# A two-layer attention kernel on one Trainium2 core: the last step's exponentials added by a transfer, a new order in layer 0, another layout of layer 1's q and k

## What is computed

```python
xn = layernorm(x)                                    # layer 0
scores = einsum('bhsd,bhtd->bhst', q, k) * scale     # q, k, v projections of xn
attn = softmax(scores, axis=-1)                      # no bias in layer 0
out = einsum('bhst,bhtd->bhsd', attn, v)             # then the projection WO[0]
x = x + out_projected * silu(ffn(xn))
xn = layernorm(x)                                    # layer 1
q, k = rope(q, c, s), rope(k, c, s)                  # halves of the head's 64 rotated
scores = einsum('bhqd,bhkd->bhqk', q, k) * SCALE
kb = -p * log1p(a * dist)
attn = softmax(scores + kb[None], axis=-1)
out = einsum('bhqk,bhkd->bhqd', attn, v)
x = x + (out @ out_w.T) * silu(experts(xn))          # top-1 of 8 experts per token
```

## Time and profile before

| | us |
|---|---|
| median of 3 runs | 2997.02 |
| lowest, highest | 2996.97, 2999.35 |
| the profiled execution | 2997.32 |
| its span, first to last instruction | 2995.6 |
| busy PE, DVE, POOL, ACT | 2729.9, 2459.0, 2458.6, 1588.5 |
| mean granted PE clock | 0.962 |

### The profile page before, as it was taken

The page is one execution under the profiler, slowest core; times in us unless marked ns, Lnnn a source line. Parts: engine busy times, 40 slices in busy tenths (PEclk is TensorE's granted clock), DMA queues, the critical chain, the costliest instruction groups (busy, mean ns, idle before and its releaser), DMA issues. The chain is left out here.

```text
span 2995.6 us, 46382 instructions
## 1 busy us (share of the span) xinstructions
PE 2729.9 (91%) x17528; PEld 1133.6 (38%) x17528; DVE 2459.0 (82%) x3309; ACT 1588.5 (53%) x1972; POOL 2458.6 (82%) x1186
## 2 busy tenths in 40 slices
PE   5959999999999999998588299999999999999996
PEld 3413333333333333333354033333333333333333
DVE  6568888888888888884566499999999999999994
ACT  3325555555555555554154155555555555555554
POOL 0009999999999999998244389999999999999997
PEclk8979999999999999999699599999999999999998
DMA  4250111111111111100323502211112121221100
GB/s 112 88 197 10 31 30 31 29 31 30 30 30 31 29 31 30 30 3 1 93 82 112 168 9 56 56 56 56 56 56 56 56 57 56 56 56 56 56 1 15
DMA packets 66063, 155.26 MB, mean 52 GB/s; under 512 B 17697, under 2 KB 31402, under 8 KB 63666
## 3 DMA queue, kind: packets, MB, share of 16 engines
q1 hardware_dynamic: 64818, 150.20, 18.0%
q0 software_dynamic: 1024, 2.10, 0.2%
HBM read 113.34 MB, written 38.93 MB: 51 GB/s over the span
## 5 line engine op out<-in xcount | busy, mean ns | idle before, releaser
L947 POOL TENSOR_TENSOR a_sums<-a_sums,room 128x1024 f32<-128x1024 f32 x512 | 1194.9, 2362 | 66.3 <-ACT room L788 42.2
L699 PE MATMUL a_ov<-room,va 128*64 128x512 f32 x4096 | 994.6, 606 | 0.0
L777 ACT ACTIVATE room<-room,sscale 128x1024 f32<-128x1024 f32 x512 | 588.8, 1150 | 504.3 <-DVE room L877 504.3
L844 DVE TENSOR_REDUCE a_mx<-a_jb 128x1 f32<-128x1024 f32 x501 | 611.8, 1221 | 128.9 <-PE a_jb L653 122.7
L947 POOL TENSOR_TENSOR a_sums<-room 128x1024 f32<-128x1024 f32 x256 | 603.2, 2357 | 76.2 <-ACT room L781 49.6
L839 DVE CUSTOM_DVE_ANT_0 a_junk<-a_jb,a_tab 128x1024 bf16<-128x1024 f32 x501 | 609.8, 1217 | 62.2 <-DVE a_m L850 36.1
L877 DVE TENSOR_TENSOR room<-a_st,a_tab 128x1024 f32<-128x1024 f32 x512 | 623.8, 1220 | 14.1 <-PE a_st L688 12.9
L788 ACT ACTIVATE room<-a_st,sscale 128x1024 f32<-128x1024 f32 x256 | 285.0, 1113 | 359.3 <-PE a_st L688 359.3
L652 PE MATMUL a_jb<-a_kh,a_qh 64*128 64x512 f16 x1002 | 387.0, 386 | 41.5 <-DVE a_mx L844 25.9
L688 PE MATMUL a_st<-a_qh,a_kh 64*128 64x512 f16 x2048 | 390.8, 378 | 0.0
L688 PE MATMUL a_st<-a_ql,a_kh 64*128 64x512 f16 x2048 | 390.0, 378 | 0.0
(11 more groups left out here) (231 smaller groups left out, 2470.3 us busy)
## 6 DMA issues: line engine op xcount, KB each, us to landing
a_tab<-bias_line SPq DMA_DIRECT2D x16, 1984.0 KB
a_qh<-qk_high SPq DMA_DIRECT2D x64, 256.0 KB, 4.5
a_kh<-qk_high SPq DMA_DIRECT2D x64, 256.0 KB, 5.0
a_ql<-qk_low SPq DMA_DIRECT2D x64, 256.0 KB, 6.6
a_kl<-qk_low SPq DMA_DIRECT2D x64, 256.0 KB, 6.8
qk_high<-q_oh SPq DMA_DIRECT2D x16, 512.0 KB, 2.6
qk_low<-q_ol SPq DMA_DIRECT2D x16, 512.0 KB, 3.6
qk_high<-er_split SPq DMA_DIRECT2D x32, 256.0 KB
```

The lines of the kernel that those rows point to most:

```text
L699: last = nc.tensor.matmul(ov[t * DH:(t + 1) * DH, :], k.va[:, 2 * s + t, h * DH:(h + 1) * DH], prob[:, step % RING, t * QC:(t + 1) * QC], ...
L777: nc.scalar.activation(prob[:, r, :], prob[:, r, :], ACT.Exp, scale=k.sscale[:, layer:layer + 1])\
L844: nc.vector.reduce_max(mx[:, j // 2, j % 2:j % 2 + 1], scratch(n, j), AX.X).then_inc(max_done, 1)
L947: nc.gpsimd.tensor_tensor(a, first, prob[:, step % RING, :], ALU.add).then_inc(summed, 1)
```

## The change

The sum of a chunk is now kept in three tiles instead of two and a total: chunks take turns with `sums[:, 0]` and `sums[:, 1]`, and `sums[:, 2]` is the second running sum of all of them. POOL adds steps 0 to 6 (five adds and the merge). Step 7's exponentials it doesn't add: it issues a transfer from the ring's tile to the sum with an accumulating write, and the fold of the chunk, now in place, waits for that transfer. The fold comes after the first add of the next chunk. A tile of step 7 may be written again when the transfer has landed (`last_added`). In layer 1 `add_part` comes after the second add and one chunk later.

SUM_STEP, ROW_STEP and OUT_STEP are 5, 3 and 7 in both layers, and ACT copies the row out one step earlier, before the exponentials of step 3. In layer 0 DVE takes the maximum ahead of the subtraction, and ACT writes `a_m4w` ahead of step 0's exponentials and copies `ov` out after them.

Layer 1's q and k lie in DRAM with all first rotation halves ahead of all second ones. A store's 128 rows are then contiguous rows; a load of a head takes 32 rows from each half, 16 transfers instead of 8. In the expert stage ACT loads each index right before its copy. `line` (of the preparation) is given back earlier, which makes room for the third sum.

```diff
-SUM_STEP, ROW_STEP, OUT_STEP = (3, 5), (5, 3), (7, 7)
+SUM_STEP, ROW_STEP, OUT_STEP = 5, 3, 7
...
+def by_halves(store):
+    return store.rearrange("a p s -> (a p) s").rearrange("(r x) s -> r x s", r=2)
+
...
-        sums, total = m.sb(g + "sums", [P, 2, 2 * QC]), m.sb(g + "total", [P, QC])
+        sums = m.sb(g + "sums", [P, 3, 2 * QC])
...
-        loads = 4 + (1 if bias else 0)
+        low_loads = 8 if bias else 4
+        loads = low_loads + (1 if bias else 0)
         FIRST = AHEAD * NJ
-        pool_adds = NS - 1
+        pool_adds = NS - 2
...
-        def summed_by(step):
+        def wait_summed(engine, step):
             n, s = divmod(step, NS)
-            return pool_adds * n + (1, 1, 2, 2, 3, 4, 5, 6)[s]
+            if s == NS - 1:
+                engine.wait_ge(last_added, 16 * (n + 1))
+            else:
+                engine.wait_ge(summed, pool_adds * n + (1, 1, 2, 2, 3, 4, 5)[s])
...
+        def placed(h):
+            pr, half = h // 2, slice((h % 2) * DH, (h % 2 + 1) * DH)
+            for low in (0, DH):
+                if not bias:
+                    yield slice(low, low + DH), lambda store: store[pr][half, :]
+                else:
+                    for r in range(2):
+                        yield (slice(low + r * DR, low + (r + 1) * DR),
+                               lambda store, r=r: by_halves(store)[r, h * DR:(h + 1) * DR, :])
...
-                    sp.wait_ge(low_loaded, 16 * 4 * h)
+                    sp.wait_ge(low_loaded, 16 * low_loads * h)
...
-                pr, half = h // 2, slice((h % 2) * DH, (h % 2 + 1) * DH)
-                for low in (slice(0, DH), slice(DH, P)):
-                    sp.dma_start(qh[low, at], k.qk_high[0, pr][half, :]).then_inc(loaded, 16)
-                    sp.dma_start(kh[low, at], k.qk_high[1, pr][half, :]).then_inc(loaded, 16)
+                for to, rows in placed(h):
+                    sp.dma_start(qh[to, at], rows(k.qk_high[0])).then_inc(loaded, 16)
+                    sp.dma_start(kh[to, at], rows(k.qk_high[1])).then_inc(loaded, 16)
                 if bias:
                     sp.dma_start(tab[:, h % 2, :], k.bias_rows(h)).then_inc(loaded, 16)
...
-                for low in (slice(0, DH), slice(DH, P)):
-                    sp.dma_start(ql[low, at], k.qk_low[0, pr][half, :]).then_inc(low_loaded, 16)
-                    sp.dma_start(kl[low, at], k.qk_low[1, pr][half, :]).then_inc(low_loaded, 16)
+                for to, rows in placed(h):
+                    sp.dma_start(ql[to, at], rows(k.qk_low[0])).then_inc(low_loaded, 16)
+                    sp.dma_start(kl[to, at], rows(k.qk_low[1])).then_inc(low_loaded, 16)
...
-                if bias and n >= 3:
+                if n >= 3:
                     pe.wait_ge(proj_done, n - 2)
-                if not bias and n >= 2:
-                    pe.wait_ge(rs_done, n - 1)
...
-                pe.wait_ge(row_done, min(n + (3 if bias else 2), NCH))
+                pe.wait_ge(row_done, min(n + 3, NCH))
                 if n >= 1:
                     pe.wait_ge(proj_done, n)
                 for q in range(4):
-                    last = nc.tensor.matmul(xb[:, q:q + 1], total[:, q * P:(q + 1) * P], k.ones[:, 0:1],
+                    last = nc.tensor.matmul(xb[:, q:q + 1], sums[:, n % 2, q * P:(q + 1) * P], k.ones[:, 0:1],
...
-                if s == row_step and n + 1 < NCH:
+                if s == ROW_STEP and n + 1 < NCH:
                     row(n + 1)
-                if s == sum_step and n >= 1:
+                if s == SUM_STEP and n >= 1:
                     sums_of(n - 1)
-                if s == out_step and n >= 1:
+                if s == OUT_STEP and n >= 1:
                     project(n - 1)
...
+                        wait_summed(act, step - RING)
...
-                    if bias and s == 0 and n + 1 < NCH:
+                    if s == 0 and n + 1 < NCH:
                         divide_maxima(n + 1)
                     exponent(n, s)
-                    if s == (0 if bias else 1) and n >= 1:
+                    if s == 0 and n >= 1:
                         copy_out(n - 1)
-                    if not bias and s == 2 and n + 1 < NCH:
-                        divide_maxima(n + 1)
-                    if s == row_step and n + 1 < NCH:
+                    if s == ROW_STEP - 1 and n + 1 < NCH:
                         row(n + 1)
-                    if bias and s == out_step and n >= 1:
+                    if bias and s == OUT_STEP and n >= 1:
                         scale(n - 1)
             copy_out(NCH - 1)
             if bias:
...
-                    ve.wait_ge(summed, summed_by(step - RING))
+                    wait_summed(ve, step - RING)
...
-                    if not by_row(NS * n + s):
-                        subtract_maxima(n, s)
                     if n + AHEAD < NCH:
                         maxima(n + AHEAD, s)
                     if bias:
                         add_bias(n, s)
-                    if s == sum_step and n >= 1:
+                    elif not by_row(NS * n + s):
+                        subtract_maxima(n, s)
+                    if s == SUM_STEP and n >= 1:
                         invert(n - 1)
-                    if not bias and s == out_step and n >= 1:
+                    if not bias and s == OUT_STEP and n >= 1:
                         accumulate(n - 1)
             invert(NCH - 1)
...
@@ -934,27 +950,37 @@
                 a = flat(k.acc[:, (n % NC) * 4:(n % NC + 1) * 4, :])
                 nc.gpsimd.tensor_tensor(a, a, part[:, :], ALU.add).then_inc(accumulated, 1)
 
+            def fold(n):
+                a = sums[:, n % 2, :]
+                pool.wait_ge(last_added, 16 * (n + 1))
+                nc.gpsimd.tensor_tensor(a[:, 0:QC], a[:, 0:QC], a[:, QC:2 * QC], ALU.add).then_inc(folded, 1)
+
             for n in range(NCH):
-                for i, s in enumerate((1, 3, 4, 5, 6, 7)):
+                a, b = sums[:, n % 2, :], sums[:, 2, :]
+                for i, s in enumerate((1, 3, 4, 5, 6)):
                     step = NS * n + s
-                    a = sums[:, (n + i) % 2, :]
+                    c = a if i % 2 == 0 else b
                     pool.wait_ge(exp_done, step + 1)
+                    if i == 0 and n >= 2:
+                        pool.wait_ge(sum_ready, n - 1)
+                    if i == 1 and n >= 1:
+                        pool.wait_ge(summed, pool_adds * n)
                     if i >= 2:
                         pool.wait_ge(summed, pool_adds * n + i - 1)
-                    if i == 1 and n >= 1:
-                        pool.wait_ge(folded, n)
-                    first = a if i >= 2 else prob[:, (step - 1) % RING, :]
-                    nc.gpsimd.tensor_tensor(a, first, prob[:, step % RING, :], ALU.add).then_inc(summed, 1)
-                pool.wait_ge(summed, pool_adds * n + 6)
-                a = sums[:, n % 2, :]
-                nc.gpsimd.tensor_tensor(a, a, sums[:, (n + 1) % 2, :], ALU.add).then_inc(summed, 1)
+                    first = c if i >= 2 else prob[:, (step - 1) % RING, :]
+                    nc.gpsimd.tensor_tensor(c, first, prob[:, step % RING, :], ALU.add).then_inc(summed, 1)
+                    if i == 0 and n >= 1:
+                        fold(n - 1)
+                    if bias and i == 1 and n >= 2:
+                        add_part(n - 2)
+                pool.wait_ge(summed, pool_adds * n + 5)
+                nc.gpsimd.tensor_tensor(a, a, b, ALU.add).then_inc(summed, 1)
+                pool.wait_ge(exp_done, NS * (n + 1))
                 pool.wait_ge(summed, pool_adds * (n + 1))
-                if n >= 1:
-                    pool.wait_ge(sum_ready, n)
-                nc.gpsimd.tensor_tensor(total[:, :], a[:, 0:QC], a[:, QC:2 * QC], ALU.add).then_inc(folded, 1)
-                if bias and n >= 1:
-                    add_part(n - 1)
+                nc.gpsimd.dma_start(a, prob[:, (NS * n + NS - 1) % RING, :], accum_op=ALU.add).then_inc(last_added, 16)
+            fold(NCH - 1)
             if bias:
+                add_part(NCH - 2)
                 add_part(NCH - 1)
...
-                rows = store[i].rearrange("a p s -> (a p) s").rearrange("(g h r d) s -> g r h d s", g=4, h=4, r=2)
-                return [rows[g, r, :, :, half * 1024:(half + 1) * 1024] for r in range(2)]
+                rows = by_halves(store[i])
+                return [rows[r, g * P:(g + 1) * P, half * 1024:(half + 1) * 1024] for r in range(2)]
...
-            owners = [act.value_load(tiles[0:1, i:i + 1], min_val=0, max_val=NE - 1) for i in range(TL)]
             act.wait_ge(weights_loaded, 16 * (1 + FT))
 
             def pick(i):
-                nc.scalar.activation(w1i[:, i % 2, :], w1[:, bass.ds(owners[i], 1), :].rearrange("p a f -> p (a f)"),
+                owner = act.value_load(tiles[0:1, i:i + 1], min_val=0, max_val=NE - 1)
+                nc.scalar.activation(w1i[:, i % 2, :], w1[:, bass.ds(owner, 1), :].rearrange("p a f -> p (a f)"),
```

(18 more changed lines are left out.)

2 lines of the change are left out of this document (1 added, 1 removed).

## The result

| | before | after |
|---|---|---|
| median | 2997.86 us | 3207.78 us |
| lowest, highest | 2996.97, 2999.35 | 3206.99, 3210.14 |
| span of the profiled execution | 2995.6 us | 3208.4 us |

The ratio is 1.0701, with a 95% interval of 1.0682 to 1.0720: the change costs 210 us. The forecast was 2964 in a range of 2900 to 3040.

What follows compares the result with a forecast made beforehand. PE and POOL (in layer 1 also DVE) were taken as near full, so waits that close a ring count. Rotation -45, ordinary chunks -16 and -12, bursts +29 and +11 gave -33: from 2997.3 to 2964 us, range 2900 to 3040.

Steps and rivals of the forecast that it cites:

- Rotation: Stage between the layers: jobs -29 us, drain -18, later bias table before layer 1 +2, together -45.
- Order: Ordinary chunks, 50 per layer: layer 0 from 18.61 to 18.3 us (-16), layer 1 from 19.53 to 19.3 (-12).
- L: The transfer's latency from its issue to the fold's start, taken as 4.9 us between bounds 4.4 and 5.7.
- the ring: POOL's path through the transfer: a chunk can't be shorter than 13.1 + L in layer 0, 14.3 + L in layer 1.
- the third rival: Both layers: L is 5.7 us even alone, so POOL's ring through the transfer becomes the bound; 3070 us, chance 0.17.
- Bursts: Chunks where a later head's loads meet the transfer, 14 per layer: +11 us in layer 0, +29 in layer 1.
- upper ends: L beside a later head's loads if all the transfer's rows take turns: 7.2 us in layer 0, 9.5 in layer 1.
- full turns: Second rival: beside a head's loads every transfer row waits its turn, layer 1 +60, layer 0 +24; 3008 us, chance 0.20.
- Ring bound: The third rival by another name: the transfer is slow even alone and bounds the chunks; 3070 us, chance 0.17.
- Hidden everywhere: First rival: the transfer is hidden in all 64 chunks of each layer, also beside loads; 2908 us, chance 0.20.
- my lower estimate of L: L taken as 4.9 us, nearer the 4.4 bound than 5.7, since reads may run beside writes in part.
- Slow stores: Fourth rival, rotation stage: stores stay slow because the engines used don't follow the rows; 3009 us, chance 0.07.

Runs made afterwards that it cites:

- POOL's own add: The changed kernel with only the transfer undone: POOL adds step 7's exponentials itself, after the merge; 2922.85 us, ratio 0.9751.
- loads held back: The changed kernel, loads of heads 2 to 15 waiting until the last chunk's transfer has landed, layer 1's bias table until the next one has; 2959.19 us.
- the run above: Changed kernel, POOL adding step 7 itself in layer 1; layer 0 keeps the transfer, loads waiting for its landing, PE's sums behind values of steps 2 and 3; 2941.51 us.
- the run with the head start: The changed kernel with loads of heads 2 to 15 issued only after the exponentials of step 1 of the next chunk; 2983.10 us, ratio 0.9942.
- the plain copy: The changed kernel whose layer 0 transfer writes plainly to the third sum's tile instead of adding to the first; 3182.0 us in a single execution.

## Why the prediction was wrong

Kernels that differ by one part of the change each give the whole:

| | step | us |
|---|---|---|
| before, to layout alone | 2997.86 to 2956.85 | -41.0 |
| to layout and order, POOL's own add | to 2922.85 | -34.0 |
| to the transfer, loads held back | to 2959.19 | +36.3 |
| to loads as in the change | to 3207.78 | +248.6 |
| sum | | +209.9 |

**Rotation, right.** Forecast -45, the +2 for layer 1's start in it, measured -41. The first load comes after 5.5 us (6). The fourteen jobs take 118.8 us and not 115: eleven at 8.41 (8.45), but the last three at 8.76, where I had taken 7.2.

**Order, right.** The version with POOL's own add has 18.32 us in layer 0 and 19.31 in layer 1; the forecast was 18.3 and 19.3. In layer 1 it is for the reason given: the row's copy alone makes its part. I counted -28 in 50 chunks of each layer, it is -34 in all of them. In layer 0 only half of the reason holds. PE's waits from 400 to 800 (in all, times, longest), first of the kernel before, then of the version with POOL's own add:

```profile
PEld a_xb L710 <- POOL a_total L954: 5.0, 21, 0.2
PE a_jb L652 <- DVE a_mx L844: 6.7, 21, 0.3
```

```profile
PEld a_xb L728 <- issue: 5.3, 22, 0.2
```

The 0.32 us at L652 is gone. The 0.24 us ahead of the sums is still there, now with no releaser, so it was not a wait for the fold, and that the number came out is in part luck.

**The transfer alone, its latency right, its ring short.** Forecast for L 4.9 us, measured 4.6 for a lone transfer and 4.8 in the mean with the loads held back. But the ring is not 13.1 + L and 14.3 + L. It is 13.5 and 14.8: 19.61 - 6.10 in the run above, and 20.67 - 5.86 in a burst of the run with the head start. What I left out is the wait of 0.55 us ahead of every issue, in which the queue waits for POOL's own merge. With 4.6 the ring is 19.4 in layer 1, over the 19.31 that the order would give, so there it binds always; the third rival was half right at a latency far below its 5.7. I had no term for what else moves L: beside a packet of the instruction queue it is half a microsecond longer in the mean and up to 1.5. Together +36, of which the folds' means show 12 in layer 0 and 19 in layer 1.

**Bursts, wrong, and this step failed.** The terms were +11 and +29; measured are 248.6. From the folds' means (20.10 against 18.45 in layer 0, 21.85 against 19.57 in layer 1, 63 chunks each) it is 104 and 144, 7.4 and 10.3 for a burst. Two things were mis-sized or missing.

First, L: 6.3 and 7.3 taken, 7.2 and 9.5 as upper ends, 10.2 and 12.3 measured. I gave POOL's packets a turn from the start. The earlier trace rows showed otherwise: a gather was issued at 1690.45, and up to 1696 only 9 of its packets ran. I read a rate out of it (turns) and not the delay. The records of the bursts give both. Of L's growth over a lone transfer (5.6 and 7.7 us) the late first packet is 2.9 and 3.3, for which the forecast had nothing. The shared engines are 2.2 and 3.6, near the 2.3 and 4.6 of "full turns", where I had taken 1.4 and 2.4. The last 0.5 and 0.8 lie between the last packet and the fold. In layer 1 I had also let part of the transfer's rows through ahead of the table; of the 71 packets that go first in the burst at 2037.27, 59 are longer than 8 KB, so the table's. The run with a head start shows what the collision costs in all: without it L is 5.1 and 5.8, at 2983 instead of 3208 us. And the plain copy shows that the cost of the packets themselves hardly counts beside it.

Second, the chunks behind the burst. The burst's own chunk is 5.4 and 7.6 us longer than with the loads held back, about as much as L has grown. The chunk behind it is 1.9 us longer in both layers; there PE works at 0.50 for 6.6 and 7.7 us in the mean, behind its wait at the sums (3.9 to 5.9 us in layer 0, 6.2 to 9.4 in layer 1). In layer 1 the next chunk is 0.8 longer too, at a granted clock of 1.00: in the one from 2070.56 to 2090.97 POOL waits for exponentials that follow DVE's adds. The forecast had no term for a clock that falls, nor for any chunk behind the burst; its rows had waits of 0.24 and 0.45 us only, which the clock survives.

**The rivals.** "Full turns in bursts" (3008) had the right place and a third of the price. "Ring bound" (3070) was the nearest in time, by another sum. "Hidden everywhere" (2908) would have needed L under 4.5 in layer 1 and is not reached by any version with a transfer. "Slow stores" is out.

**Rules beside rows.** The Trainium skill ("Collectives: The Full Stack", on why ReduceScatter is half of AllGather) says that an add reads twice where a copy reads once. The packets agree, 0.35 against 0.16 us, yet the lone landing grows only from 2.9 to 4.6 us, so my lower estimate of L was the better one. The Trainium skill ("DMA: Bandwidth & Descriptors", on queues, rings and completion order) says that an engine drains a whole packet before it turns to another queue, and that such a packet holds some 9 to 17 descriptors. I took it for one row, because the profile calls a row a packet. By the page as it stands a transfer typically waits for 9 to 17 of them on each engine. In the burst shown 266 packets of the profile, 17 per engine, ran in the first 4 us. Without those of the first 1.5 us, in which a lone transfer's packets don't run either, 9 to 14 per engine went first in layer 0's bursts. That agrees. Layer 1's first 3.8 us have only 71 packets, 4 per engine, which the count does not explain.

**What stays open.** Whether the first 4 us are such a drained packet, rows that the engines had taken in already, or a transfer that is itself late to reach them: the records don't name the engine, and all three give way to a head start. That the lower clock makes the 1.9 us of the chunk behind the burst is read from the stretches and not shown, since no run kept the clock up through a burst. Why a single instruction packet holds a transfer up by up to 1.5 us was not tried.

## What to carry to other kernels

Here the add that POOL handed to a transfer was paid back at the first wait for its landing. Put the latency, with the wait ahead of the issue, into the ring before counting the saved work, and compare the sum with the engine's own 2.33 us. If the queues are shared with big loads, ask who is issued first; moving the loads by 5.3 us in layer 0 and 6.5 in layer 1 decided about 225 us here. And price a wait of the matrix engine at more than its length, since behind 1.2 us of it the clock can fall.

## What the runs showed of the hardware that was not expected

- A 128 x 1024 f32 accumulating transfer inside SBUF runs its 4 KB packets in 0.35 us, a plain one in 0.16; landings 4.6 and 2.9 us.
- Issued 3.2 us behind the first load its first packet comes 3.8 to 4.9 us after the issue in layer 0, issued 5.5 us behind it 4.0 to 5.7 in layer 1; ahead of them 1.5, as alone. After that it shares the engines half and half.
- A PE wait of 1.17 us was followed by 3 us at the lower clock in 33 chunks and not in 27 others with the same wait, in an order that I can't explain; one of 4.28 us by 6 us.
- A transfer with an instruction packet beside it lands half a microsecond later in the mean (5.09 against 4.63 us from issue to fold), 1.5 at most.
